# Graph attention on one core: low parts of Wk made by GpSimd, more filler matmuls behind the first transposes, and new orders

## The reference

```python
h = jnp.maximum(_layernorm(x, axis=-1), 0.0)          # x: 64 graphs x 128 nodes x 384
q = _heads(h @ Wq + bq); k = _heads(h @ Wk + bk); v = _heads(h @ Wv + bv)    # 6 heads of 64
scores = jnp.einsum('bhqd,bhkd->bhqk', q, k) / np.sqrt(HEAD_SIZE)
bias = jnp.where(adj, 0.0, NEG)[:, None]
probs = jax.nn.softmax(scores + bias, axis=-1)
ctx = jnp.einsum('bhqk,bhkd->bhqd', probs, v)
return x + (ctx @ Wf + bf)
```

## Time and profile before

| | |
|---|---|
| median of 3 executions | 466.36 us (464.83 to 466.47) |
| profiled execution, its own time | 467.61 us |
| span of the profiled execution, first to last instruction | 465.6 us |
| TensorE busy | 457.8 us, 98% of the span |
| VectorE, ScalarE, GpSimd busy | 361.9 us (78%), 364.6 us (78%), 309.2 us (66%) |
| mean granted TensorE clock | 0.996 |

### The profile page before, as it was taken

How to read it: one execution, slowest core, us unless ns; L and a number is a source line. 1 busy time by engine, 2 the same in 40 slices (tenths; PEclk the granted TensorE clock), 3 DMA queues, 4 the chain that set the end, 5 groups by cost and what they waited for, 6 DMA issues and landing times.

```text
span 465.6 us, 12837 instructions
## 1 busy us (share of the span) xinstructions
PE 457.8 (98%) x4459; PEld 273.2 (59%) x4459; DVE 361.9 (78%) x726; ACT 364.6 (78%) x822; POOL 309.2 (66%) x339
## 2 busy tenths in 40 slices
PE   6999999999999999999999999999999999999997
PEld 3764656565565655656565565655656565565565
DVE  5899977868696886968779696885868778686875
ACT  5679999886879699695977969489786967986770
POOL 4179486965866848587585857758577484775670
PEclk9999999999999999999999999999999999999999
DMA  8257789997995989969497795949969889699497
GB/s 299 69 75 182 108 164 128 246 157 183 203 193 134 194 180 160 211 135 215 120 210 163 161 216 120 206 103 181 195 151 163 190 148 211 118 181 171 114 171 218
DMA packets 219758, 78.55 MB, mean 169 GB/s; under 512 B 199488, under 2 KB 219712, under 8 KB 219712
## 3 DMA queue, kind: packets, MB, share of 16 engines
q1 hardware_dynamic: 209344, 65.63, 72.3%
q10 hardware_dynamic: 10368, 12.33, 10.1%
HBM read 16.19 MB, written 12.58 MB: 62 GB/s over the span
## 4 chain that ended last, share of the span: by engine, by line
PE 85%; ACT 4%; DVE 3%; POOL 3%; DMA 2%; issue 2%; SPq 1%; ACTq 0%; POOLq 0%
PE ps L1092 26%; PE ps L1093 26%; PE ps L1094 26%; PE ps L1154 6%; DMA ct_parts<-ctx_parts 2%; ACT masked L819 1%; POOL probs_parts L720 1%; SPq L631 1%; POOL x_bf L715 1%; DMA x_sb<-in_x 1%; ACT probs_parts L834 1%; DVE masked L935 1%; ACT qkt_hi L805 1%; ACT h_sb L796 0%; DVE stats L892 0%
## 5 line engine op out<-in xcount | busy, mean ns | idle before, releaser
L720 POOL TENSOR_TENSOR probs_parts<-masked,probs_parts 128x768 f16<-128x768 f32 x64 | 104.9, 1647 | 59.6 <-ACT probs_parts L834 59.4
L819 ACT ACTIVATE masked<-masked,neg_max 128x128 f32<-128x128 f32 x384 | 118.4, 390 | 15.4 <-DVE neg_max L944 14.1
L1092 PE MATMUL ps<-ht_parts,w_hi 128*128 128x512 f16 (+1 forms) x315 | 111.9, 361 | 0.4 <-DVE masked L935 0.4
L1093 PE MATMUL ps<-ht_parts,w_hi 128*128 128x512 f16 (+1 forms) x315 | 111.9, 361 | 0.0
L1094 PE MATMUL ps<-ht_parts,w_lo 128*128 128x512 f16 (+1 forms) x315 | 111.9, 361 | 0.0
L916 DVE SCALAR_TENSOR_TENSOR qkt_lo<-ps,bias_qk,qkt_hi 128x512 f16<-128x512 f32 x96 | 68.4, 743 | 17.5 <-ACT qkt_hi L805 17.5
L715 POOL TENSOR_TENSOR x_bf<-x_sb,b_out 128x384 f32<-128x384 f32 x64 | 63.4, 1003 | 20.9 <-DVE y_sb L974 20.8
L726 POOL TENSOR_TENSOR ctx_parts<-ctx_sb,ctx_parts 128x384 f16<-128x384 f32 x62 | 56.5, 916 | 25.2 <-ACT ctx_parts L840 24.8
L805 ACT ACTIVATE qkt_hi<-ps,bias_qk 128x512 f16<-128x512 f32 x96 | 62.7, 679 | 13.2 <-PE ps L1094 12.0
L935 DVE SCALAR_TENSOR_TENSOR masked<-ps,score_unscale,mask 128x384 f32<-128x384 f32 x128 | 70.8, 608 | 1.8 <-PE ps L1154 1.3
L1092 PE MATMUL ps<-w_hi,ct_parts 128*128 128x384 f16 (+1 forms) x195 | 63.2, 324 | 0.4 <-DVE v_lo L922 0.2
(11 more groups left out here) (95 smaller groups left out, 902.5 us busy)
## 6 DMA issues: line engine op xcount, KB each, us to landing
x_sb<-in_x ACTq DMA_DIRECT2D x56, 192.0 KB, 2.8
y<-y_sb SPq DMA_DIRECT2D x56, 192.0 KB, 2.4
x_sb<-in_x SPq DMA_DIRECT2D x8, 192.0 KB, 5.6
y<-x_bf SPq DMA_DIRECT2D x7, 192.0 KB, 3.8
pt_parts<-probs_parts SPq DMA_TRANSPOSE x64, 4.0
ct_parts<-ctx_parts SPq DMA_TRANSPOSE x62, 3.0
adj_sb<-in_adj ACTq DMA_DIRECT2D x14, 64.0 KB, 2.5
w_raw<-in_Wk SPq DMA_DIRECT2D x1, 576.0 KB, 6.0
```

The source lines that it names most:

```text
L720: nc.gpsimd.tensor_tensor(probs_parts[b][:, 1, :], probs[b], probs_parts[b][:, 0, :], ALU.subtract).then_inc(probs_split, 1)
L819: last = nc.scalar.activation(masked[b][:, u, :], masked[b][:, u, :], ACT.Exp, bias=neg_max[b][:, u:u + 1])
L1092: nc.tensor.matmul(to, a_hi, b_hi, start=first, stop=False)
L1093: nc.tensor.matmul(to, a_hi, b_lo, start=False, stop=False)
```

## The change

For Wk the low parts move from VectorE to GpSimd, in two instructions a slice: GpSimd multiplies the raw weight by the scale into `w_scaled`, and then subtracts `w_hi`. `w_scaled` is the buffer that ScalarE fills for Wf later on, so `weight_scaled` now waits until Wk's slices are done. The second call of `keep_busy` issues four matmuls where it issued one. The tables of turns are written anew for all groups, and one output of group 13 goes to bank 3 where it went to bank 0.

```diff
-REST_BY_VECTOR = (0, 1, 2)
-KEEP_BUSY = (9, 1, 1)
+REST_BY_VECTOR = (0, 2)
+SCALED_BY_GPSIMD = (1,)
+KEEP_BUSY = (9, 4, 1)
...
     if stage in ("weight_scaled", "weight_lo", "weight_rest"):
-        return group > 0 or (item // C in REST_BY_VECTOR) != (stage == "weight_rest")
+        return (group > 0 or (item // C in REST_BY_VECTOR) != (stage == "weight_rest")
+                or stage == "weight_scaled" and item // C in SCALED_BY_GPSIMD)
...
     13: {
-        "project_out": (6, 7, 6, 0),
+        "project_out": (6, 7, 6, 3),
...
             def weight_lo(group, item, i):
                 n, c = divmod(item, C)
+                if n in SCALED_BY_GPSIMD:
+                    pool.wait_ge(scale_step, SCALE_STEPS * (n + 1))
+                    nc.gpsimd.tensor_tensor(w_scaled[c][:], w_raw[n][:, c, :], w_scale[:, n:n + 1].broadcast_to([P, H]),
+                                            ALU.mult).then_inc(w_scaled_ready[n], 1)
                 pool.wait_ge(w_hi_ready[n], c + 1)
...
                 act.wait_ge(scale_step, SCALE_STEPS * (n + 1))
-                if item >= C:
-                    act.wait_ge(w_split[n - 1], c + 1)
+                for other in SCALED_BY_GPSIMD:
+                    act.wait_ge(w_split[other], c + 1)
...
-    "normalize_ctx": (230, 10000, 10140, 10180), "mask_scores": (10, 20, 70, 80), "largest_score": (30, 60, 90, 130),
-    "values_lo": (40, 110, 120, 170), "finish": (10190, 10200, 10310, 20050),
+    "mask_scores": (0, 20, 60, 90), "normalize_ctx": (220, 10010, 10140, 10190), "largest_score": (30, 50, 80, 130),
+    "finish": (10200, 10210, 10310, 20040), "values_lo": (70, 100, 110, 160),
```

More of the change, by code:

```diff
@@ L181 @@
[L181 to L184 removed]
+        "project_qk": (-9930, -9910, -9880, -9850, -9830, -9820), "project_v": (-9750, -9740, -9730, -9720),
+        "scores": (-9790, -9780, -9770), "weigh_values": (-9630, -9590, -9510, -9460),
@@ new lines @@
+        "statistics": (-29750, -29720, -19900, -19890), "aggregate": (-19880,),
+        "qk_lo": (-19490, -19470, -19460, -19440, -19430, -19420), "additive_mask": (-19390,),
+        "values_lo": (-19310, -19260, -19230, -19170), "mask_scores": (-19380, -19360, -19350, -19330),
+        "largest_score": (-19370, -19340, -19300, -19280), "normalize_ctx": (-19120, -19070, -18950, -18840),
+        "finish": (-18830, -18820, -18710, -18610), "qk_hi": (-19590, -19560, -19550, -19480, -19470, -19450),
@@ L202 @@
+        "transpose_normed": (-19880, -19870), "transpose_ctx": (-19570, -19560, -19500, -19490),
+        "store": (-19520, -19400, -19390, -19380),
     },
     13: {
-        "project_qk": (-29540, -29520, -29510, -29470, -29430, -29400),
-        "project_v": (-29330, -29320, -29260, -29250), "scores": (-29370, -29360, -29350),
-        "weigh_values": (-29200, -29170, -29080, -29070), "project_out": (-29030, -28980, -28960, -28910),
-        "statistics": (-29590, -29560, -29550, -29530), "aggregate": (-29510,), "additive_mask": (-29290,),
@@ new lines @@
+        "project_v": (-29330, -29320, -29270, -29260), "scores": (-29370, -29360, -29350),
+        "weigh_values": (-29210, -29180, -29060, -29040), "project_out": (-29030, -28980, -28960, -28900),
+        "statistics": (-29570, -29550, -29540, -29530), "aggregate": (-29520,),
+        "qk_lo": (-29180, -29150, -29140, -29100, -29090, -29080), "additive_mask": (-29250,),
+        "values_lo": (-29010, -28930, -28890, -28860), "mask_scores": (-29050, -29040, -29000, -28940),
+        "largest_score": (-29020, -28990, -28980, -28800), "normalize_ctx": (-28790, -28750, -28600, -28590),
@@ new lines @@
+        "statistics": (-39270, -39240, -39220, -39200), "aggregate": (-39190,),
+        "qk_lo": (-38970, -38870, -38850, -38780, -38770, -38760), "additive_mask": (-39110,),
+        "values_lo": (-38740, -38660, -38620, -38380), "mask_scores": (-38730, -38720, -38680, -38670),
+        "largest_score": (-38700, -38690, -38650, -38640), "normalize_ctx": (-38530, -38520, -38430, -38350),
+        "finish": (-38360, -38310, -38300, -38250), "qk_hi": (-39020, -38980, -38940, -38860, -38850, -38840),
@@ L237 @@
+        "transpose_probs": (-39450, -39430, -39360, -39330), "transpose_normed": (-39630, -39620),
+        "transpose_ctx": (-39340, -39310, -39300, -39270), "store": (-39200, -39190, -39180, -39170),
     },
     15: {
-        "project_qk": (-49090, -49060, -49050, -49040, -49020, -48990),
-        "project_v": (-48890, -48880, -48860, -48810), "scores": (-48970, -48950, -48930),
-        "weigh_values": (-48850, -48820, -48790, -48780), "project_out": (-48770, -48740, -48730, -48720),
-        "turn_ctx": (-48760, -48750), "statistics": (-48960, -48930, -48920, -48890), "aggregate": (-48880,),
@@ L254 @@
-        "transpose_probs": (-49310, -49280, -49270, -49250), "transpose_normed": (-49500, -49490),
-        "transpose_ctx": (-49240, -49230, 10050, 10080), "store": (-49160, -49150, -49140, -49130),
+        "project_qk": (-49100, -49090, -49080, -49050, -49020, -48990),
+        "project_v": (-48910, -48880, -48860, -48810), "scores": (-48970, -48950, -48940),
+        "weigh_values": (-48850, -48820, -48800, -48770), "project_out": (-48760, -48740, -48730, -48720),
+        "turn_ctx": (-48780, -48750), "statistics": (-48960, -48920, -48910, -48900), "aggregate": (-48880,),
```

311 lines of the change are left out of this document (148 added, 163 removed).

## The result

The changed kernel takes 468.08 us (median of 22 executions, 467.06 to 469.68) where the kernel before takes 466.24 (22 executions on the same chip, 464.83 to 469.24): ratio 1.0031, 95% interval 1.0017 to 1.0045. It is 0.3% slower by the ratio, and 1.84 us by the medians. The forecast was 465.1 us, with 462.9 to 467.4 as range: the direction is wrong, and the time lies outside.

A forecast was written before the change was run, and what follows sets the result against it. TensorE was taken as full at its upper clock, leaving 21.3 us outside the steady groups to win or lose; -1.0 (start) + 0 (GpSimd) + 0.3 - 0.6 + 0 = -1.3 us gave 465.1 us, range 462.9 to 467.4.

The forecast's parts named there:

- Loop and end: Groups from the loop to the last output: TensorE's order same or calls exchanged among themselves; 0, with 0.4 us either way.
- The sum, and what it was held against: Whole kernel: terms sum to -1.3 us, taken from the profiled execution, then set against the median of three, 466.36 us.
- the main term: Start of the kernel: held clock and new order bring K's projection earlier; 1.0 us gain, bounds 0.2 and 1.3.
- Fillers hold the clock: Start, TensorE's 1.92 us wait: five matmuls there keep the full clock behind it, saving 1.70 us less matmul time.
- the clock falls anyway: Rival, at the start: the clock drops despite fillers, start gives 0.2 instead of 1.0, 465.9 us; chance 0.15.
- GpSimd and VectorE's relief: Wk's low parts, early: GpSimd's six instructions cost nothing, multiplication 1.00 us; VectorE's 1.66 us saved is worth nothing by itself.
- 42 us: Group 0's fourth mask, now behind other instructions, frees TensorE's bank late: 0.3 us loss, bounds 0 and 0.8.
- 93 and 102 us: Two TensorE waits there, shortened by handling V earlier: 0.6 of 1.0 us won back, bounds 0 and 1.0.
- V's low part late in the loop: Rival: first graph's `values_lo` makes TensorE wait 0.9 us in each of six loop groups, 470.5 us; chance 0.12.

The follow-up runs named there:

- the execution with the clock held: The kernel before, unchanged, profiled again: 465.89 us, with a granted clock of 1.00 at the start.
- the moved mask: Changed kernel with the making of group 12's additive mask moved about 5 us earlier on VectorE: 467.25 us, ratio 1.0020 to the kernel before.
- the V moves: Kernel before with the third group's V copied and split earlier, and the next group's additive mask earlier: 466.75 us, ratio 1.0003.
- the fillers alone: Kernel before with five filler matmuls instead of two, between the first two graphs' transposes: 465.97 us, ratio 0.9983.

## Why the prediction was wrong

**Loop and end.** The larger error is in the step "I take 0, with 0.4 either way". The trace shows a loss of 2.4 us there against the trace that was read, 0.25 in the loop and 2.15 behind it, and 2.56 against the execution with the clock held, the last stores included in both. For the late groups the step went by the calls being the same ones and the last output's chain as it was; what now stands in front of the instruction that frees TensorE's next bank, it asked at one place of the loop alone. In the loop one `scores` call in each of three passes loses 0.17 us instead of 0.09, behind a weight load that waits for `qk_lo`. The 0.37 at 333.66 us does not come in the kernel with the moved mask, whose order there is the same, so not every execution has it. About 1.0 is lost at 358 us (shown by the moved mask), the rest at 379 and 451 us and behind the start of the last `project_out` (0.58). That the late tables make the late loss is shown by exchanging them. At the very end, the two half stores take longer from issue to landing. That more stores are still under way just ahead of them may be why, which no run tested. Median us to landing, changed kernel, then the kernel before in the execution with the clock held:

```profile
y<-x_bf SPq DMA_DIRECT2D x2, 96.0 KB, 2.2
```

```profile
y<-x_bf SPq DMA_DIRECT2D x2, 96.0 KB, 1.8
```

**The sum, and what it was held against.** The other step that fails is "It lies 1.25 us above the median of the three executions, 466.36; against that the forecast is 465.1 us". The profiled execution was longer than the median because its clock had fallen at the start, and the main term, 1.0 us, was the cost of that fall. It was counted as a gain and then taken off a median in which most executions don't have it: a clock that always holds is worth 0.2 to 0.9 us there. Against the execution with the clock held, the start with the change is 0.48 us later, not 1.0 earlier. This step alone does not account for the miss: with nothing for the start the sum is -0.3, and 466.1 us would still be 2.0 too low.

**A wait that no term held.** At 35 us TensorE waits for the transposed h of the second group. The last two of four transposes are issued at the same times (28.5 and 29.9 us; before, with the clock held, 28.3 and 30.0) and land later, at 34.1 and 34.8 us instead of 32.6 and 33.2. DMA issues of that stretch, median us to landing, changed and then before:

```profile
ht_parts<-h_pairs SPq DMA_TRANSPOSE x2, 5.2
```

```profile
ht_parts<-h_pairs SPq DMA_TRANSPOSE x2, 3.7
```

The same matmul of TensorE in that execution of the kernel before, which has no wait in front of it:

```profile
33.84 0.38 PE L1092 MATMUL ps<-ht_parts,w_hi 128*128 128x512 f16 x1
```

In the trace that was read these had 0.4 us to spare at 35.58 us; a TensorE that comes 1.3 us earlier needed them earlier, and the prediction did not ask for their landing. Why they are slower stays open. It is not the first group's table alone: with the old one they took 4.9 and 4.3 us. Nor is it the changed tables alone: with Wk's low parts back on VectorE and a late x they were issued at 32.0 and 33.3 us and took 4.2 and 3.6.

**Fillers hold the clock.** The mechanism is right in the main, and was counted for more than it gives. With the new order at the start and four fillers, 2 of 68 executions have a mean clock of 0.996 (the changed kernel 0 of 22, three experiments 1 of 11, 0 of 12 and 1 of 11, the moved mask 0 of 12); with the same order and one filler it is 1 of 11; with TensorE's old start and all else changed, 6 of 11; the kernel before has 33 of 91. So it matters that some matmuls stand in the wait, and as far as these runs tell, two do as well as five. They do not exclude a fall: in the traces of two kernels with five matmuls there, x landed late, TensorE waited 2.36 and 2.47 us all the same, and the clock fell. The rival "the clock falls anyway" had the reason why the gain shrinks, that executions differ, but asked it of the changed kernel only; most executions of the kernel before have no fall to win back. Near this lies a statement of the Trainium skill, page "TensorE: Matmul & The Clock Gate", section "What's actually happening": the number of slow matmuls at a kernel's start differs from run to run of the same kernel. These runs show the like for a fall that comes later: 0.50, 0.66 and 1.00 in the same window of the same program.

**GpSimd and VectorE's relief.** Right: hidden, and worth nothing that can be told (467.82 us with the move undone, 468.08 with it). The multiplication was taken 0.17 us too long, on the safe side: the output type, which the prediction let decide, does not, for the multiplication into float32 (0.83) is shorter than the subtraction into float16 (0.92).

**42 us.** Wrong, and small: 0.3 us was put there, and nothing is lost. The mask ended at 42.25 us and TensorE wanted its bank at 42.89.

**93 and 102 us.** Right in kind, too small: 0.6 forecast, 1.04 and 1.25 found (against the two executions of before in the table). TensorE's matmul at the second place, 100.60 us in the execution of before with the clock held, now has no wait in front of it:

```profile
100.46 0.19 PE L1099 MATMUL ps<-v_hi,pt_parts 128*128 128x65 f16 x1
```

**V's low part late in the loop.** Did not come: 27.8 us a group in the loop, as before (28.0 from group 4 to 14, with the waits behind the loop).

Held against the execution of 465.89 us, the whole account is: start +0.48, 35 us +0.80, up to 55 us -0.17, 93 and 102 us -1.25, up to the loop +0.13, loop +0.25, late groups +1.71, end +0.60, together +2.55; the own times differ by 2.65. The medians differ by 1.84: that of before lies 0.35 above its execution, because it is taken over executions with a fall as well, and that of the changed kernel 0.46 below.

No version here beats both kernels by what can be measured. The kernel before stays the best by its median, with the V moves and the fillers alone as candidates that single traces and the counts of falls speak for.

## What to carry to other kernels

Before pricing a loss that a profile shows, ask whether every execution has it: where the profiled time lies above the median, the difference may be that very loss, and a gain against it must not be subtracted from the median. Where each execution's mean clock is on record, it counts how often a fall happens, which one or two traces can't: here the single traces of the kernels with one filler and with five would make fillers look useless. Orders that are rewritten as a whole are to be priced as a whole: with TensorE full for 98% of the span, a reshuffle can win little and lose anywhere, and every place where an instruction of 1 us moves in front of the one that frees TensorE's next bank is a place to look. A table of lost time at equal work shows in ten lines what two different orders win and lose where.

## What the runs showed of the hardware

The same program starts differently from execution to execution. The x of the second and third graph landed at 5.6 and 6.3 us in one trace of the kernel before, at 7.4 and 8.0 or 5.8 and 8.1 in traces of kernels with the same loads, and over the kernels of this case K's start moved between 17.35 and 21.93 us. An idle time of TensorE of about 2 us at the start is followed by the lower clock in some executions and not in others (1.92, 2.29: fell; 2.26, 2.27: held). With matmuls on constants in that wait and 0.50 to 1.30 us left idle, five traces show no fall. A DMA transpose took from 2.7 to 7.1 us from issue to landing in the changed kernel's trace, with no row that says which it will be. GpSimd multiplies 128 by 384 float32 by one broadcast number for each row in 0.83 us, less than an addition of two full tiles (1.01).
